# Spectral layer: ScalarE copies the second part's own products, VectorE takes its pair products from PSUM, and one matrix remainder moves a unit later on GpSimd

## The reference

```python
U_plus = irfft(Vf[None, :, :, None] * Uf_p[:, :, None, :], n=n, axis=1)[:, :sl]
U_minus = irfft(Vf[None, :, :, None] * Uf_m[:, :, None, :], n=n, axis=1)[:, :sl]
U_minus = U_minus * sgn[None, :, None, None]
...
s = sigma ** SIGMA_POW
out = jnp.einsum('btkd,k,kde->bte', U_plus, s, Mpp)
out = out + jnp.einsum('btkd,k,kde->bte', U_minus, s, Mpm)
```

## Time and profile before

| | us |
|---|---|
| median of 3 runs | 7693.79 (7692.5 to 7694.76) |
| profiled execution, whole time | 7697.52 |
| its span | 7695.5 |
| TensorE busy in the span | 6986.6 (91%) |
| VectorE busy | 6292.1 (82%) |
| ScalarE busy | 4533.2 (59%) |
| GpSimd busy | 4643.8 (60%) |
| L2500, the mixing, TensorE busy | 523.4 |
| L2605 on VectorE, 256 times, busy | 277.8 |
| L2620 on VectorE, 256 times, busy | 162.4 |

### The profile page before, as it was taken

One profiled execution on the slowest core, in us unless ns is written; L12 is line 12 of the kernel. 1 busy time (PEld: TensorE's weight loads), 2 busy tenths in 40 slices (PEclk: granted clock), 3 DMA queues, 4 the chain that ended last, 5 costly groups with the idle time before them and its releaser, 6 DMA issues. The chain is left out here.

```text
span 7695.5 us, 180193 instructions
## 1 busy us (share of the span) xinstructions
PE 6986.6 (91%) x64774; PEld 5968.0 (78%) x64774; DVE 6292.1 (82%) x9149; ACT 4533.2 (59%) x9445; POOL 4643.8 (60%) x5010
## 2 busy tenths in 40 slices
PE   8999989999899998999957999888879989899898
PEld 6888768888588885888836888546648989889898
DVE  7999879998799997999945777556668878888788
ACT  5888658887588874888811333325554545545454
POOL 5888748887388882888817766222114545445454
PEclk9999999999999999999969999889989999999999
DMA  2333213332133331323347776200004434344343
GB/s 64 91 92 92 86 53 92 92 93 85 53 91 92 92 86 51 94 90 94 91 131 233 231 200 190 75 3 23 11 20 134 131 114 133 106 134 131 114 133 106
DMA packets 595164, 774.81 MB, mean 101 GB/s; under 512 B 52215, under 2 KB 528408, under 8 KB 592193
## 3 DMA queue, kind: packets, MB, share of 16 engines
q1 hardware_dynamic: 542529, 594.11, 26.0%
q0 software_dynamic: 51840, 169.91, 7.5%
HBM read 730.16 MB, written 33.66 MB: 99 GB/s over the span
## 5 line engine op out<-in xcount | busy, mean ns | idle before, releaser
L647 POOL TENSOR_TENSOR l_arena<-l_arena 128x768 f32<-128x768 f32 x1536 | 2596.6, 1691 | 450.3 <-DVE l_arena L579 444.2
L579 DVE TENSOR_TENSOR_SCAN l_arena<-l_arena,psum 128x772 f32<-128x772 f32 x1536 | 2662.8, 1750 | 176.7 <-PE psum L406 72.6
L500 ACT ACTIVATE l_arena<-l_arena,l_A 128x384 f32<-128x384 f32 x3072 | 1643.0, 603 | 38.2 <-DVE l_arena L579 32.8
L408 PE MATMUL psum<-l_arena 128*128 128x128 f32 x11520 | 1500.6, 280 | 45.6 <-DVE l_arena L579 41.9
L408 PEld LDWEIGHTS psum<-l_arena 128*128 128x128 f32 x11520 | 1368.6, 193 | 169.2 <-issue 145.4
L419 PE MATMUL psum<-l_ident,l_arena 128*128 128x128 f32 x9216 | 1257.6, 273 | 50.6 <-ACT l_yT L506 41.7
L419 PEld LDWEIGHTS psum<-l_ident,l_arena 128*128 128x128 f32 x9216 | 1055.2, 141 | 60.2 <-POOL l_arena L647 60.2
L2683 POOL TENSOR_TENSOR st_U<-st_Uc,st_U 128x384 f16<-128x384 f32 x512 | 470.7, 919 | 839.0 <-ACT st_U L2649 839.0
L1211 POOL DMA_INDIRECT l_G<-neighbours,l_idx x648 | 622.3, 960 | 391.6 <-issue 189.9
L490 ACT ACTIVATE l_arena<-l_arena,l_BT 128x256 f32<-128x256 f32 x1728 | 746.8, 496 | 7.5
L2500 PE MATMUL psum<-st_U,st_W 128*128 128x128 f16 (+3 forms) x6144 | 523.4, 226 | 44.6 <-POOL st_U L2683 35.2
(11 more groups left out here) (469 smaller groups left out, 11981.1 us busy)
## 6 DMA issues: line engine op xcount, KB each, us to landing
l_arena<-c_rows SPq DMA_DIRECT2D x1536, 192.0 KB, 3.0
st_FS<-filter_sums SPq DMA_DIRECT2D x128, 1155.0 KB, 9.1
st_F<-filter_parts SPq DMA_DIRECT2D x128, 320.5 KB, 6.8
neighbours<-l_xt SPq DMA_DIRECT2D x256, 72.0 KB
st_mab<-in_st_mp SPq DMA_DIRECT2D x68, 256.0 KB, 9.3
st_mab<-in_st_mm SPq DMA_DIRECT2D x68, 256.0 KB, 6.6
l_G<-neighbours,l_idx POOLq DMA_INDIRECT x648, 3.7
l_arena<-in_x SPq DMA_DIRECT2D x4, 1152.0 KB, 5.2
```

The costliest lines, as they stand in the source:

```text
L408: mm = pe.matmul(ps[:, o:o + P], dtuT[:, g % 2, t, h * P:(h + 1) * P], diagB[:, rank[s] % 3, t, :], start=True, stop=True)
L500: act.activation(decay[:, s % NDC, half(h)], dtv[:, g % 2, h, :], ACT.Exp, scale=A[:, g // NRC, h, n:n + 1]).then_inc(s_exp, 1)
L579: dve.tensor_tensor_scan(hbuf[:, n, run], decay[:, s % NDC, run], x2_ps[s % 2][:, run], 0.0, ALU.mult, ALU.add).then_inc(s_scan, 1)
L647: pool.tensor_tensor(hC[:, s % NHC], halves(hbuf[:, s % NS, :]), Cs[:, s % NCS, :].unsqueeze(1).broadcast_to([P, 2, RC]), ALU.mult).then_i ...
```

## The change

Four edits stand in the diff. ScalarE copies the second part's OWN products into `second` (the tile `Uc`) instead of the PAIR products into `pair_1`, and no longer waits for VectorE before it. VectorE's add and its two subtractions read PAIR straight from PSUM. TensorE, which overwrites PAIR at L2540, waits for VectorE's second subtraction (`s_ed`, done + 5) instead of ScalarE's copy (`s_ea`, copied + 4). And GpSimd makes the matrix remainder for z = 1 in unit 1 instead of unit 0.

```diff
-        kept = xr[:].rearrange("p q x -> p (q x)")[:, 0:6 * RC].rearrange("p (n x) -> p n x", n=6)
-        own_s, pair_s, pair_1, pair_2 = kept[:, 0:2, :], kept[:, 2:4, :], kept[:, 4, :], kept[:, 5, :]
+        kept = xr[:].rearrange("p q x -> p (q x)")[:, 0:5 * RC].rearrange("p (n x) -> p n x", n=5)
+        own_s, pair_s, pair_2 = kept[:, 0:2, :], kept[:, 2:4, :], kept[:, 4, :]
...
-                            pe.wait_ge(s_ea, copied + 4)
+                            pe.wait_ge(s_ed, done + 5)
                             pairs(u, FS[:, :, :, :, 1], 0, True).then_inc(s_cv, 1)
...
-                            dve.tensor_tensor(second, ps[:, OWN:OWN + RC], pair_1, ALU.add).then_inc(s_ed, 1)
+                            pair_ps = ps[:, PAIR:PAIR + RC]
+                            dve.tensor_tensor(second, second, pair_ps, ALU.add).then_inc(s_ed, 1)
                             dve.wait_ge(s_ed, at + 3)
-                            dve.tensor_tensor(second[:, P:], second[:, P:], pair_1[:, 0:2 * P], ALU.subtract).then_inc(s_ed, 1)
-                            dve.tensor_tensor(second[:, 0:P], second[:, 0:P], pair_1[:, 2 * P:], ALU.subtract).then_inc(s_ed, 1)
+                            dve.tensor_tensor(second[:, P:], second[:, P:], pair_ps[:, 0:2 * P], ALU.subtract).then_inc(s_ed, 1)
+                            dve.tensor_tensor(second[:, 0:P], second[:, 0:P], pair_ps[:, 2 * P:], ALU.subtract).then_inc(s_ed, 1)
...
                             act.wait_ge(s_cv, (unit + u) * 6 + 4)
-                            act.wait_ge(s_ed, (unit + u) * 12 + 17)
-                            act.activation(pair_1, ps[:, PAIR:PAIR + RC], ACT.Copy).then_inc(s_ea, 1)
+                            act.activation(Uc[:, 0, :], ps[:, OWN:OWN + RC], ACT.Copy).then_inc(s_ea, 1)
...
-                            if u % NU == 0:
+                            if u % NU == 1:
                                 mixing_low(b * each + (i * 2 + r) * 2 + 2, r, 1)
```

## The result

The changed kernel takes 7576.08 us (median; 7573.19 to 7583.02), the kernel before beside it 7693.15 (7688.24 to 7694.76): a ratio of 0.9848, interval 0.9836 to 0.9861. The profiled execution took 7573.19, its span is 7571.1, its granted clock 0.964.

A forecast was written before the change was run, and what follows sets the result against it. TensorE was taken as the bound, so only its waits could be won. Per filter 3 x 0.03 + 1.19 - 0.65 = 0.63 us, times 64, gave 40.3 us and a median of 7653.5; range 7605 to 7680.

The forecast's parts named there:

- The two subtractions: VectorE's subtractions reading PSUM: the 256-wide one takes 0.42 us, not held by GpSimd; VectorE gains 0.64 per unit.
- The rule against the change: Skill page's higher PSUM latency on VectorE: 0.065 us per subtraction, 33 us in all, leaving about 7687.
- The rival with PSUM inputs held by GpSimd: VectorE's 256-wide subtraction stays at 1.06 us, a unit takes 7.16, 86 us slower: 7780; chance 0.09.
- The matrix remainder: GpSimd's remainder leaving unit 0 ends the stall from unit 1 to 2: 7.70 to 6.51, a gain of 1.19 per filter.
- What is late next: End of unit 1: GpSimd's remainder comes 0.16 before edge operation L2600, which waits; unit 2's add is late, 0.65 lost per filter.
- the sign that the prediction named against itself: Edge operation L2600 on VectorE staying at 0.28 us would show the forecast wrong.
- the rival "no collision": Unit 1: L2600 gets ahead of GpSimd because L2581 waits less; 1.28 gained per filter, 82 us: 7612; chance 0.18.
- The term of 0.65: Loss per filter, in us, from VectorE's edge operation L2600 waiting for GpSimd's remainder and delaying unit 2's add.
- ScalarE's copy: Copying OWN instead of PAIR keeps its 0.49 us, starting 0.33 after `third`; the dropped, long-met `s_ed` wait changes nothing.
- TensorE's new wait: Third part's pair matmuls wait 0.27 us for the second subtraction, starting at 2.13; ordinary unit 6.54 to 6.52, 6.51 used.
- The sum: All units of a filter: 3 x 0.03 + 1.19 - 0.65 = 0.63 us gained, times 64, 40.3 us.

The follow-up runs named there:

- the run with the zeros: Changed kernel plus one 0.27 us VectorE write of zeros per filter, behind unit 1's last weight step: 7624.22 us, ratio 0.9909 against the kernel before.

## Why the prediction was wrong

Read by its steps, with 64 filters:

- *The two subtractions*: right. 0.42 with GpSimd running, 421 ns over all 256. The rule against the change (the Trainium skill, "VectorE: DVE Perf Modes", section "The TRN2 errata — SBUF-src ops pay a fixed extra latency per instruction") is not seen here: the PSUM form is 421 ns, the SBUF form 425. The rival with PSUM inputs held by GpSimd is refuted by the same row.
- *The matrix remainder*: right. L2569 at 0.68, the long unit gone. Taken back it costs 0.72 per filter, not 1.19: the subtractions alone had already brought the long unit from 7.70 to 7.12, so the two edits share this gain, which the prediction put down to the move.
- *What is late next*: **the step that failed.** L2600 was put 1.41 behind the 256-wide step from the earlier trace rows, as if VectorE's own work set that distance. It did not. Before, the edge operations had to wait for ScalarE's copy of `low_s`, which the prediction weighed for GpSimd and not for them. Timeline of ScalarE and VectorE, kernel before:

```profile
7340.59 0.60 ACT L2645 ACTIVATE st_low_s<-psum 128x512 f32<-128x512 f32 x1 [0.85 <-PE psum L2465]
...
7341.22 0.29 DVE L2599 TENSOR_TENSOR st_low_s<-st_low_s 128x128 f32<-128x128 f32 x1
```

The copy ends at 7341.19 and L2599 starts at 7341.22, 0.66 behind the start of the weight step (7340.56); in the changed kernel it starts 0.52 behind it (the step at 7238.14, L2599 at 7238.66), for the copy (L2646) has ended at 7238.24. Counted to `third` of the next unit, the copy ends 0.17 ahead of it in both kernels (7341.36, 7238.41), while the 256-wide step went from 1.34 ahead to 0.82, just where the prediction had it (6.51 - 5.69): by its own times `low_s` was ready before the edge operations. With `low_s` ready the distance is 1.27, so GpSimd's 1.26 is ahead by 0.01 and not by 0.16, and L2600 stays at 0.28, the sign that the prediction named against itself. The margin decided, as the rival "no collision" said with 0.18; its reason (L2581 waits less) was not the one that acted. The term of 0.65 falls away: 42 us.
- *ScalarE's copy*: the second miss, a term of zero that was 0.08 us a unit. "The dropped wait on `s_ed` was long met" was true and the conclusion not: standing behind an unmet wait it was paid for every time. The copy starts at 0.25 instead of 0.33, *TensorE's new wait* is 0.18 instead of 0.27, and the pairs start at 2.04 instead of 2.13.
- *TensorE's new wait* was right in kind. With the wait put back the ordinary unit is 6.47, the forecast 6.51 (its terms add up to 6.52): 0.04 was missed here. What the shown idle of 0.29 was worth to the unit was taken as 0.29; the block behind a wait is shorter in the rows (0.51 against 0.55). Whether that is all of it stays open.
- *The sum*: A filter takes 25.57 instead of 27.30 - 0.63 = 26.67: 1.10 x 64 = 70 us on top of the 40, which makes the 111 of the filters. The 6 that are left of 117 (12 of 122.5 in the later run of the changed kernel) fit the shorter ScalarE list, 7 to 10, which the prediction did not look for.

The Trainium skill, "SBUF — State Buffer", section "SBUF: two separate sides", says that of a VectorE operation with two SBUF inputs and a GpSimd operation the one that starts first holds the shared port for the whole instruction. Both orders are in the rows: GpSimd held to 1.07 by L2600 in the changed kernel, VectorE held to 1.00 behind GpSimd when the 0.27 were added. But which of two is first cannot be read to the last tenth from where their rows begin. GpSimd began 0.01 ahead of L2600, and in the run with the zeros 0.08 ahead of the first edge operation (7226.96, 7227.04), and both times it was GpSimd that was held (1.07, 1.08); where it began 0.14 ahead of L2605 and 0.22 ahead of L2601, VectorE was. Where between 0.08 and 0.14 this turns stays open.

## What to carry to other kernels

When a margin of a tenth decides between two engines, look up for each distance taken from the trace what set it there, and ask whether that is still last after the change; a distance that was a wait is not one that can be carried over. Put the wait that is met early ahead of the one that is met late, or leave it out. And an edit that moves a stall is worth trying together with the one that shortens the engine it moves to: the move alone gave 0.58 us a filter, where the whole stall was 1.16.

## What was not expected of the hardware

- A second wait that is long met costs ScalarE about 0.06 to 0.08 us if it stands behind the unmet one (copy at 0.33 after `third`, against 0.27 and 0.25), and nothing in the filter's interval if it stands ahead (25.57 both).
- 16 rows more on ScalarE's list, waits or copies, turned 256 instruction transfers into 272 and made ScalarE wait 11.2 us instead of 6.7 between images, 7 to 10 us in all. Why just there was not tried.
- A two-SBUF-input operation on VectorE got in ahead of a GpSimd operation whose row began 0.01 us before its own (L2600 at 7238.86, GpSimd at 7238.85), and 0.2 us later it lost 0.72: 48 us hang on it. That it follows directly on another such operation is not what saves it: with the move alone L2606 (7229.93) follows directly on L2605, GpSimd began 0.24 ahead of it (7229.69), and L2606 was held to 1.00.
